# Layer 2 attention of a hybrid conv/attention kernel: keys masked by head only, score products over 32 rows and 512 columns

## What is computed

```python
q = _rope(proj(wq, lora_A_q, lora_B_q).reshape(B, S, N_HEADS, HEAD_DIM), cos, sin).transpose(0, 2, 1, 3)
k = _rope(proj(wk, lora_A_k, lora_B_k).reshape(B, S, N_HEADS, HEAD_DIM), cos, sin).transpose(0, 2, 1, 3)
v = proj(wv, lora_A_v, lora_B_v).reshape(B, S, N_HEADS, HEAD_DIM).transpose(0, 2, 1, 3)
scores = jnp.einsum('bhqd,bhkd->bhqk', q, k) * INV_SQRT_HD
scores = jnp.where(causal[None, None], -jnp.inf, scores)
attn = jax.nn.softmax(scores, axis=-1)
out = jnp.einsum('bhqk,bhkd->bhqd', attn, v).transpose(0, 2, 1, 3).reshape(B, S, DIM) @ wo.T
```

## Time and profile before

| | us |
|---|---|
| median of 3 runs | 774.87 (772.77 to 777.02) |
| span of the profiled execution (the page gives no other time for it) | 775.8 |
| PE busy, share | 566.2, 73% |
| PE weight loads | 324.7, 42% |
| DVE busy | 340.6, 44% |
| ACT busy | 336.1, 43% |
| L573 products of parts 1 and 2, 128 records | 35.3 |
| L569 products of part 0, 128 records | about 19 |
| Layer 2's attention loop | some 233 to 351 us of the span |

### The profile page before, as it was taken

One profiled execution on the slowest core, in us unless ns is written; L12 is line 12 of the kernel. 1 busy time (PEld: TensorE's weight loads), 2 busy tenths in 40 slices (PEclk: granted clock), 3 DMA queues, 4 the chain that ended last, 5 costly groups with the idle time before them and its releaser, 6 DMA issues. The chain is left out here.

```text
span 775.8 us, 10987 instructions
## 1 busy us (share of the span) xinstructions
PE 566.2 (73%) x4080; PEld 324.7 (42%) x4081; DVE 340.6 (44%) x734; ACT 336.1 (43%) x1095; POOL 0.2 (0%) x4
## 2 busy tenths in 40 slices
PE   6665566567877999986566666665899998995463
PEld 5322222235645766664333333333455544551321
DVE  2170000049757788875200000006887546776233
ACT  2233333337737677772333333334544465442121
POOL 0000000000000000000000000000000000000000
PEclk9755555559997999997555555558999999997577
DMA  4000000000000000000000000004000000000000
GB/s 166 1 1 1 1 0 1 1 0 1 3 0 1 2 1 2 2 1 1 1 1 1 0 1 1 0 1 108 1 2 1 1 1 1 2 1 0 8 5 27
DMA packets 4954, 6.73 MB, mean 9 GB/s; under 512 B 1186, under 2 KB 4642, under 8 KB 4772
## 3 DMA queue, kind: packets, MB, share of 16 engines
q1 hardware_dynamic: 4900, 6.01, 2.5%
HBM read 3.38 MB, written 0.52 MB: 5 GB/s over the span
## 5 line engine op out<-in xcount | busy, mean ns | idle before, releaser
L303 PE MATMUL ps<-arena,wsb 16*16 16x16 f32 (+1 forms) x1024 | 131.5, 206 | 111.1 <-ACT arena L321 111.1
L321 ACT ACTIVATE arena<-ps 16x16 f32<-16x16 f32 (+1 forms) x512 | 96.3, 188 | 199.3 <-PE ps L303 199.3
L303 PEld LDWEIGHTS ps<-arena,wsb 16*16 16x16 f32 (+1 forms) x1024 | 76.4, 118 | 196.2 <-ACT arena L321 191.7
L327 DVE TENSOR_TENSOR X<-X,ps 128x128 f32<-128x128 f32 x16 | 4.6, 288 | 206.6 <-PE ps L288 206.6
L965 ACT ACTIVATE arena<-ps 128x512 f32<-128x512 f32 x96 | 56.6, 597 | 62.0 <-PE ps L726 60.7
L1267 DVE TENSOR_TENSOR arena<-arena,ps 128x512 f32<-128x512 f32 x96 | 64.0, 685 | 41.2 <-ACT arena L965 24.9
L744 PE MATMUL ps<-arena 128*32 128x128 f32 x768 | 60.3, 279 | 7.3 <-DVE arena L1267 7.3
L889 ACT ACTIVATE arena<-ps,arena 128x128 f32<-128x128 f32 (+1 forms) x128 | 52.4, 418 | 29.9 <-DVE arena L1140 29.8
L744 PEld LDWEIGHTS ps<-arena 128*32 128x32 f32 x768 | 34.8, 109 | 41.9 <-DVE arena L1267 22.6
L1139 DVE TENSOR_REDUCE arena<-ps 128x2 f32<-128x512 f32 (+1 forms) x48 | 33.0, 688 | 18.6 <-PE ps L569 11.1
L586 PE MATMUL ps<-wsb,arena 128*128 128x128 f32 x192 | 30.4, 282 | 11.6 <-DVE arena L1148 11.5
(11 more groups left out here) (231 smaller groups left out, 805.8 us busy)
## 6 DMA issues: line engine op xcount, KB each, us to landing
arena<-xn SPq DMA_DIRECT2D x16, 128.0 KB, 2.5
wsb<-weights SPq DMA_DIRECT2D x1, 1916.5 KB, 8.8
wsb<-weights SPq DMA_DIRECT2D x1, 549.5 KB, 4.8
X<-x SPq DMA_DIRECT2D x1, 512.0 KB, 3.9
out<-X SPq DMA_DIRECT2D x1, 512.0 KB, 3.0
csb<-consts SPq DMA_DIRECT2D x1, 160.0 KB, 8.8
arena<-w SPq DMA_DIRECT2D x2, 64.0 KB
arena<-b SPq DMA_DIRECT2D x4, 0.5 KB
```

Of the source, the lines that this page charges most:

```text
L303: nc.tensor.matmul(step_columns(k, rows, r), w_state, states[0:rows, :, :, t].rearrange("p g j -> p (g j)"), start=False, stop=True, skip_ ...
L321: nc.scalar.activation(states[0:rows, :, :, t + 1].rearrange("p g j -> p (g j)"), step_columns(t // STEP_BANK, rows, t % STEP_BANK), func) ...
```

## The change

The masked copies are made by head only: four copies instead of sixteen, copy h holding in all groups the 8 rows of head h. The group is picked by contracting only over its 32 rows: both operands are sliced at partitions 32g to 32g + 32. All heads of a unit then go into one product of 512 columns. DVE makes the copies of heads 0 to 2 after the rotation, ACT that of head 3, and PE waits for all of them once, ahead of unit 0. Helper functions name the unit's batch, part and slot; they give the same order and slots as the arithmetic that they replace. `head_mask` (16 columns) becomes `head_rows` (4 columns) among the weights.

```diff
-        kz = at(G * HEADS, J, T)
+        kz = at(HEADS, J, T)
+        def l2_unit(u):
+            return u // 3, u % 3
+        def l2_last_unit(b):
+            return 3 * b + 2
+        def l2_slot(b, part):
+            return (3 * b + part) % 6
+        def l2_batch_ending(u):
+            return u // 3 if u >= 0 and u % 3 == 2 and u < UNITS else None
...
# PE
+            pe.wait_ge(s["L2 keys"], 2)
             for u in range(UNITS + 5):
                 if u < UNITS:
-                    b, part = u // 3, u % 3
+                    b, part = l2_unit(u)
                     j, g = b // G, b % G
-                    if b < G and part == 0:
-                        pe.wait_ge(s["L2 keys"] if g % 2 else s["L2 keys scalar"], g // 2 + 1)
+                    rows = slice(C * g, C * g + C)
                     if u >= 3:
                         pe.wait_ge(s["L2 exp"], u - 2)
-                    bank = ps[:, part, :]
+                    bank = ps[:, u % 3, :]
                     if part == 0:
                         nc.tensor.matmul(bank, CB("identb"), CB("mask_above").unsqueeze(1).to_broadcast([P, HEADS, P]),
                                          start=True, stop=False)
-                        for h in range(HEADS):
-                            mm = nc.tensor.matmul(bank[:, h * P:(h + 1) * P], q[:, j, 0:P], kz[:, g * HEADS + h, j, 0:P],
-                                                  start=False, stop=(h == HEADS - 1))
+                        mm = nc.tensor.matmul(bank, q[rows, j, 0:P], kz[rows, :, j, 0:P], start=False, stop=True)
                     else:
-                        for h in range(2):
-                            nc.tensor.matmul(bank[:, h * T:(h + 1) * T], q[:, j, P:T],
-                                                  kz[:, g * HEADS + 2 * (part - 1) + h, j, :], start=(h == 0), stop=False)
+                        nc.tensor.matmul(bank, q[rows, j, P:T], kz[rows, 2 * (part - 1):2 * part, j, :], start=True, stop=False)
...
# ACT
-            def keys_scalar(g): ...
-            keys_scalar(0)
+            nc.scalar.activation(kz[:, 3, :, :].rearrange("p j t -> p (j t)"), qk[:, 1, :], ACT.Copy,
+                                 scale=W("head_rows")[:, 3:4]).then_inc(s["L2 keys"], 1)
...
-                if u == 1:
-                    keys_scalar(2)
...
-                        act.wait_ge(s["L2 pv"], v // 3 - 1)
+                        act.wait_ge(s["L2 pv"], l2_unit(v - 6)[0] + 1)
...
# DVE
-            def keys_vector(g): ...
+            for h in range(3):
+                ins = nc.vector.tensor_scalar(kz[:, h, :, :].rearrange("p j t -> p (j t)"), qk[:, 1, :],
+                                              W("head_rows")[:, h:h + 1], None, ALU.mult)
+            ins.then_inc(s["L2 keys"], 1)
             for u in range(UNITS + 6):
-                if u == 1:
-                    keys_vector(1)
-                if u == 4:
-                    keys_vector(3)
...
# packing of the weights
-    put("head_mask", np.repeat(np.eye(G * HEADS), HD, axis=0))
+    put("head_rows", np.tile(np.repeat(np.eye(HEADS), HD, axis=0), (G, 1)))
```

More of the change, by code:

```diff
@@ L62 @@
     ("L2_A_q", P), ("L2_A_k", P), ("L2_A_v", P), ("L2_B_qT", P), ("L2_B_kT", P), ("L2_B_vT", P),
-    ("cos", T), ("sin", T), ("head_mask", G * HEADS), ("L2_wo_by_head", C),
+    ("cos", T), ("sin", T), ("head_rows", HEADS), ("L2_wo_by_head", C),
     ("F_WT", P), ("F_VT", P), ("F_gamma", 1), ("F_beta", 1), ("avg_g", P),
@@ L588, in _ @@
                     mm.then_inc(s["L2 turned"], 1)
-                if u >= 5 and (u - 5) % 3 == 0 and (u - 5) // 3 < B:
-                    b = (u - 5) // 3
+                b = l2_batch_ending(u - 3)
+                if b is not None:
                     j, g = b // G, b % G
-                    pe.wait_ge(s["L2 turned saved"], 3 * (b + 1))
+                    pe.wait_ge(s["L2 turned saved"], l2_last_unit(b) + 1)
                     if b >= 2:
@@ L600, in _ @@
                             mm = nc.tensor.matmul(ps[C * h:C * h + C, 6 + b % 2, qt * P:(qt + 1) * P],
-                                                  vt[:, j * TT + kt, C * g:C * g + C], prob6[:, (3 * b + part) % 6, c0:c0 + P],
+                                                  vt[:, j * TT + kt, C * g:C * g + C], prob6[:, l2_slot(b, part), c0:c0 + P],
                                                   start=(kt == 0), stop=(kt == qt))
                     mm.then_inc(s["L2 pv"], 1)
-                if u >= 7 and (u - 7) % 3 == 0:
-                    b = (u - 7) // 3
+                b = l2_batch_ending(u - 5)
+                if b is not None:
                     pe.wait_ge(s["L2 attended"], b + 1)
@@ L879, in _ @@
             for u in range(UNITS + 2):
-                if u == 1:
-                    keys_scalar(2)
                 if u < UNITS:
-                    heads, width = (HEADS, P) if u % 3 == 0 else (2, T)
+                    heads, width = (HEADS, P) if l2_unit(u)[1] == 0 else (2, T)
                     act.wait_ge(s["L2 minus max"], u + 1)
@@ L1119, in _ @@
                 dve.wait_ge(s["L2 rotated"], i + 1)
[L1121 to L1126, removed]
+            for h in range(3):
+                ins = nc.vector.tensor_scalar(kz[:, h, :, :].rearrange("p j t -> p (j t)"), qk[:, 1, :],
+                                              W("head_rows")[:, h:h + 1], None, ALU.mult)
+            ins.then_inc(s["L2 keys"], 1)
             for u in range(UNITS + 6):
-                if u == 1:
-                    keys_vector(1)
-                if u == 4:
-                    keys_vector(3)
                 if u < UNITS:
-                    heads = HEADS if u % 3 == 0 else 2
+                    heads = HEADS if l2_unit(u)[1] == 0 else 2
                     dve.wait_ge(s["L2 scores"], u + 1)
@@ L1143, in _ @@
                     v = u - 1
-                    heads = HEADS if v % 3 == 0 else 2
+                    heads = HEADS if l2_unit(v)[1] == 0 else 2
                     dve.wait_ge(s["L2 exp"], v + 1)
@@ L1149, in _ @@
                                             .to_broadcast([P, heads, HALF // heads]), ALU.mult).then_inc(s["L2 probabilities"], 1)
-                if u >= 6 and (u - 6) % 3 == 0 and (u - 6) // 3 < B:
-                    b = (u - 6) // 3
+                b = l2_batch_ending(u - 4)
+                if b is not None:
                     dve.wait_ge(s["L2 pv"], b + 1)
@@ L1156, in _ @@
                     nc.vector.tensor_copy(oat[:, (b % G) * T:(b % G + 1) * T], ps[:, 6 + b % 2, 0:T]).then_inc(s["L2 attended"], 1)
-                if u >= 8 and (u - 8) % 3 == 0:
-                    b = (u - 8) // 3
+                b = l2_batch_ending(u - 6)
+                if b is not None:
                     dve.wait_ge(s["L2 out"], b + 1)
```

## The result

| | before | after |
|---|---|---|
| median of the runs, us | 775.94 (4 runs) | 784.13 (4 runs) |
| ratio to before, 95% interval | | 1.0105 [1.0062, 1.0148] |
| span of the profiled execution | 775.8 | 782.2 |
| first rotation product to last addition of the attention | 126.4 | 130.4 |

The change costs 1.05%, where -0.5% was forecast. The profiled execution of after lies at 784.02, 1.8 over its span; in the prediction I had no such figure for before and put its span against the median as it stood.

A forecast was written before the change was run, and what follows sets the result against it. Bound: a steady 6.60 us loop where PE's order ties with DVE and ACT, plus key-copy gaps at the start. Start -6.5 and shape changes +2.6 make -3.9, rounded to -3.8: 771.1 us, range 767 to 779.

The forecast's parts named there:

- Key copies, the part on the engines: Start of Layer 2's attention: 16 copies become 4; PE starts 0.5 us later, gaps of 2.40 and 2.63 us go.
- both stalls: PE's waits at the stage's start, 2.40 us before 240.51 and 2.63 before 249.80; forecast to go.
- Key copies, the clock: At the start, half-clock time behind the two gaps goes: 1.5 and 1.7 us of the gross 8.2 won.
- Width: In the score products: 128 become 48, columns streamed unchanged; at most 0.03 us a batch won, taken as 0.
- Changes of shape: Steady batches, 32-row score products beside 128-row neighbours: 0.12 us a change, 0.17 a batch, 2.6 lost over 15 repeats.
- the slack that I took off: At the PV products of a steady batch: PE less than 0.1 us late to be last; 0.07 taken off.
- the loop: Steady batch, 6.60 us: part 0's scores, two tying paths (DVE and ACT, or PE's order), PV, part 0 again.
- The rule on mode changes: At changes between 32 and 128 rows: by the skill's rule each drains TensorE and would cost 0.28 us.
- full drain: Rival, steady batches: 0.28 us a change makes PE the bound, +0.75 a batch, total 779.6; chance 0.16.
- the clock falls: Rival, attention stage: chip grants 1.2 GHz for 32-row products, 70 us over the stage, partly 20 to 40; chance 0.12.
- The sum: Whole kernel: start -6.5 us, changes of shape +2.6, together -3.9, rounded to -3.8; forecast 771.1; chance 0.52.

The follow-up runs named there:

- the stall: Changed kernel with eight added DVE copies ahead of unit 24's maximum, so PE stands mid-stage: ratio to before 1.0454; the same edit in the kernel before: 1.0149.

## Why the prediction was wrong

- *Key copies, the part on the engines: right.* First mask product 0.6 later than before (0.5 said), both stalls gone, and 7.0 us won in three batches when the rows are 128.
- *Key copies, the clock: this is the step that failed.* I wrote "5.0 if the clock after the new, 3.7 us long idle time stays low some 1.5 us longer" and so took the return of the clock as a matter of time once PE works. In these runs it depended on what PE works on. With 32-row products it came after 20 us (27 and 44 in two other executions) instead of 3 to 4, and that took back 7.1 us in three batches (26.4 against 19.3 with 128 rows), of which the period explains 3 x 0.29 = 0.9.
- *Width: nearly right.* 0.04 a batch where the bound was 0.03 and I took 0.
- *Changes of shape: right in place, kind and price; the slack that I took off was not there.* On the loop 0.25 a batch against before, 0.17 said. From part 2's product to its mask 1.05 (0.97 before), which is 0.08; from the mask of part 0 to its product 0.32 (0.22) and from there to the maximum 1.16 (1.09), since the product's own load now starts with it, which is 0.17. Together 0.25, and two changes at 0.12 are 0.24. But I had taken 0.07 off for PE being that much ahead of ACT at the products with the values. From part 2's product to them it takes 1.70 now and 1.61 before, so they moved with PE, and PE had no slack. Over the twelve steady batches 3.1 us. Against the 6.56 that the same products give with 128 rows it is 0.29.
- *The rule on mode changes.* The Trainium skill, "TensorEngine Tiling (Array Packing)", Key Properties, says that a change of tiling mode drains TensorE. The trace agrees that a change costs, 0.08 and 0.17 at the two on the loop. The 0.28 that I had worked out for a full drain did not show; the rival "full drain" asked for 7.35 us a batch, and 6.85 was measured.
- *The rival "the clock falls"* had the mechanism and 0.12. I had priced it as a fall in the steady part, 20 to 70 us, and argued it away by pointing to the recurrences' waits. It came where the pipeline fills, at some 6 us, and in the steady part in some executions only (two falls in the run with 128 rows in the first four batches, one more behind the stall). The range had it outside because the case was left out as a whole, and the upper end of 779 was set by the drain.
- *The sum*: for the start and the first three batches -6 was forecast and +0.7 measured (9.5 + 26.4 against 8.9 + 26.3); for the steady batches +2.6 in fifteen was forecast and +3.1 in twelve measured; the tail gave +0.3.

## What to carry over

Slicing an operand down to 32 rows saves masked copies, but not PE time: a product takes as long, its neighbours' loads come out from under it, and here TensorE sat at 1.2 GHz for 20 to 44 us although it was never idle. Before counting on a recovered clock, look at what PE will be fed when it recovers; a stretch of full busy share at 0.50 is the sign. Where groups must be told apart, masking the stationary side by group and the moving side by head keeps all 128 rows with 8 copies instead of 16.

## What the runs showed of the hardware

- Fourteen f32 products of 512 columns in a row: 12.2 us with 128 rows, 12.3 with 64, 20.6 with 32, since the clock fell 4 us after the first. Behind 3.1 us of idle time: 23.7 with 64 rows and 23.9 with 32, at 1.2 GHz throughout; the 128-row products of the stage behind them had 2.4 GHz back some 4 us after their first.
- In the stage itself 32-row products with 128-row transposes, masks and value products between them ran at either level for tens of us: 86 us at 1.00, and up to 44 us at 0.50 with PE busy all the time. What tipped it one way or the other in an execution is open.
- A change between 32 or 64 and 128 rows shows the next load: the load queue stands 0.17 ahead of the score products of part 1 and 0.23 ahead of those of part 0, where it stands not at all with 128 rows, and 0.76 ahead of the mask behind a score product, where it stands 0.24 with 128. Six small products of another column shape a batch moved the period only from 6.56 to 6.60.
